# Linear attention and feed-forward joined into one stage by 512 tokens, with the low half of the feed-forward's inner rows on GpSimd

## The reference

```python
# linear attention, 16 heads of 16, over the 64 rows of a sequence
q, k, v = relu(x @ Wq.T + bq), relu(x @ Wk.T + bk), x @ Wv.T + bv
kv    = einsum('bnhd,bnhp->bhdp', k, v)
denom = maximum(einsum('bnhd,bhd->bnh', q, k.sum(axis=1)), 1e-6)
y     = einsum('bnhd,bhdp->bnhp', q, kv) / denom + x
out   = (y - mean(y)) / sqrt(var(y) + 1e-5) * gamma + beta
# feed-forward, 768 inner rows, int weights times 1/127
h   = silu(x @ (w_gate / 127).T) * (x @ (w_up / 127).T)
out = h @ (w_down / 127).T
```

## Time and profile before

| | us |
|---|---|
| median of 3 runs | 2300.51 (2300.44 to 2300.74) |
| the profiled execution's own time | 2298.4 |
| its span, first to last instruction | 2296.7 |
| TensorE busy | 2145.7 (93%) |
| VectorE busy | 1202.0 (52%) |
| ScalarE busy | 1066.5 (46%) |
| GpSimd busy | 483.7 (21%) |
| mean granted TensorE clock | 0.969 |

### The profile page before, as it was taken

The page is one execution under the profiler, slowest core; times in us unless marked ns, Lnnn a source line. Parts: engine busy times, 40 slices in busy tenths (PEclk is TensorE's granted clock), DMA queues, the critical chain, the costliest instruction groups (busy, mean ns, idle before and its releaser), DMA issues. The chain is left out here.

```text
span 2296.7 us, 51145 instructions
## 1 busy us (share of the span) xinstructions
PE 2145.7 (93%) x21377; PEld 1876.0 (82%) x21377; DVE 1202.0 (52%) x3545; ACT 1066.5 (46%) x2411; POOL 483.7 (21%) x365
## 2 busy tenths in 40 slices
PE   6999999999999997845979999999999899999999
PEld 6888989898988896424857888878989889898898
DVE  6655555555555554485345778862786532313311
ACT  4545444545444543203226666653444344444443
POOL 1000000000000000102011212223454454545544
PEclk9999999999999998977989999998999999999999
DMA  4100000000000000000031111010101011011000
GB/s 138 29 20 15 20 15 20 15 20 20 15 20 15 20 2 21 4 11 31 1 102 30 31 30 30 12 39 1 56 1 38 1 38 37 1 38 37 1 10 28
DMA packets 48805, 58.12 MB, mean 25 GB/s; under 512 B 6529, under 2 KB 40129, under 8 KB 48449
## 3 DMA queue, kind: packets, MB, share of 16 engines
q1 hardware_dynamic: 48576, 54.85, 7.6%
HBM read 46.72 MB, written 2.10 MB: 21 GB/s over the span
## 5 line engine op out<-in xcount | busy, mean ns | idle before, releaser
L797 POOL TENSOR_TENSOR moe_h<-moe_hr,moe_h 128x512 fp32r<-128x512 f32 x256 | 361.4, 1412 | 428.0 <-ACT moe_hr L1109 428.0
L1108 ACT ACTIVATE moe_h<-bank,dec_b 128x512 fp32r<-128x512 f32 x256 | 176.4, 689 | 418.9 <-PE bank L83 415.8
L2092 DVE TENSOR_REDUCE lat_neg_max<-bank 128x1 f32<-128x320 f32 x256 | 113.6, 486 | 319.0 <-PE bank L1873 319.0
L83 PE MATMUL bank<-lat_wv,lat_kv_t 128*128 128x256 f32 (+1 forms) x1728 | 264.8, 303 | 10.3 <-ACT lat_v L1967 3.9
L83 PE MATMUL bank<-lat_kv_t,lat_wk 128*128 128x320 f32 x1536 | 256.3, 316 | 0.0
L83 PEld LDWEIGHTS bank<-lat_wv,lat_kv_t 128*128 128x128 f32 x1728 | 224.1, 190 | 33.7 <-ACT lat_v L1967 5.7
L83 PEld LDWEIGHTS bank<-lat_kv_t,lat_wk 128*128 128x128 f32 x1536 | 225.8, 188 | 0.1
L1463 DVE SCALAR_TENSOR_TENSOR x_sb<-bank,moe_xs,x_sb 128x256 f32<-128x256 f32 x96 | 39.8, 477 | 352.0 <-PE bank L966 351.9
L83 PE MATMUL bank<-dec_xt,dec_lo 128*128 128x512 f32 x512 | 202.6, 396 | 0.0
L1981 ACT ACTIVATE lat_p<-bank,lat_neg_max 128x320 f32<-128x320 f32 x256 | 137.0, 535 | 114.0 <-DVE lat_neg_max L2092 114.0
L1569 POOL TENSOR_TENSOR lat_rs_rstdc<-lat_rs_varc,lat_rs_halfc 128x4 f32<-128x4 f32 x16 | 16.2, 1014 | 765.8 <-DVE lat_rs_varc L1561 765.8
(11 more groups left out here) (316 smaller groups left out, 3954.3 us busy)
## 6 DMA issues: line engine op xcount, KB each, us to landing
raw_w<-in_L_ffn_W SPq DMA_DIRECT2D x16, 1024.0 KB, 6.5
lat_ctx_raw<-in_ctx SPq DMA_DIRECT2D x16, 512.0 KB, 4.1
att_ctx_raw<-in_ctx_turned SPq DMA_DIRECT2D x16, 512.0 KB, 3.8
lat_kv_t<-lat_lt SPq DMA_DIRECT2D x32, 128.0 KB, 2.2
out_x<-x_sb SPq DMA_DIRECT2D x4, 512.0 KB, 2.9
x_sb<-in_x SPq DMA_DIRECT2D x1, 1792.0 KB, 14.7
lat_xl_now<-lat_xl SPq DMA_DIRECT2D x7, 256.0 KB, 4.5
lat_raw<-in_L_xattn_Wq SPq DMA_DIRECT2D x1, 1024.0 KB, 7.5
```

The costliest lines, as they stand in the source:

```text
L83: mm = pe.matmul(out, lhs(a, k), rhs(b, k), start=first and k == 0 and n == 0, stop=last and k == KD - 1 and n == 2)
L797: pool.tensor_tensor(h[:, g % 2, 1, :], hr[:, g % 2, :], h[:, g % 2, 0, :].bitcast(F32), ALU.subtract).then_inc(h_lo, 1)
L1108: act.activation(h[:, n % 2, 0, :], h_bank[n % 2][:, :], ACT.Relu, bias=bias).then_inc(h_hi, 1)
L2092: dve.tensor_reduce(neg_max[:, u:u + 1], s_bank[h][:, 0:LK], AX.X, ALU.max, negate=True).then_inc(s_max, 1)
```

## The change

The two stages become one, `linear_feed`. It goes by chunks of four tiles (`PER` = 4, 512 tokens). While chunk c goes through linear attention, chunk c-1 goes through the feed-forward; the last chunk's feed-forward comes at the end alone. The barrier between the stages goes. Every engine's queue is written anew:

```diff
...
+            sp.dma_start(wi[:, :, 0, :], rows(w["L0_ffn_w_gate"])).then_inc(ffn_loads, 16)
+            sp.dma_start(wi[:, :, 1, :], rows(w["L0_ffn_w_up"])).then_inc(ffn_loads, 16)
+            sp.dma_start(wdi[:, :, :], rows(w["L0_ffn_w_down"])).then_inc(ffn_loads, 16)
...
         @block.gpsimd
...
+            def hidden_low(c, h):
+                n = c * NH + h
+                pool.wait_ge(h_hi, n + 1)
+                pool.tensor_tensor(ht[:, 1, h, :], hf[:, n % 2, :], ht[:, 0, h, :].bitcast(F32),
+                                  ALU.subtract).then_inc(h_lo, 1)
+            power_and_shift(norm_l, shift_l, l_shift, 0)
+            pool.wait_ge(ffn_loads, 48)
+            pool.tensor_scalar(wf[:, :], wi[:, :], 1.0 / 127.0, None, ALU.mult).then_inc(gu_float, 1)
             pool.wait_ge(loads, 128)
-            pool.wait_ge(front.xn_ready, NT)
-            pool.tensor_tensor(x_sb[:, :, :], x_sb[:, :, :], beta[:, :].unsqueeze(1).to_broadcast([P, NT, D]),
-                               ALU.add).then_inc(beta_added, 1)
-            pool.wait_ge(consts, 3)
-            norm2.power(pool, 0)
+            add_beta(0)
+            pool.tensor_scalar(wdf[:, :], wdi[:, :], 1.0 / 127.0, None, ALU.mult).then_inc(wd_float, 1)
+            low_weights_up()
+            power_and_shift(norm_l, shift_l, l_shift, 1)
+            norm_y.power(pool, 0)
+            power_and_shift(norm_f, shift_f, f_shift, 0)
+            low_weights_down()
+            for c in range(1, NCH):
+                add_beta(c)
+                for h in range(PER):
+                    hidden_low(c - 1, h)
+                    if h == 1 and c + 1 < NCH:
+                        power_and_shift(norm_l, shift_l, l_shift, c + 1)
+                norm_y.power(pool, c)
+                hidden_low(c - 1, PER)
+                hidden_low(c - 1, PER + 1)
+                power_and_shift(norm_f, shift_f, f_shift, c)
+            for h in range(NH):
+                hidden_low(NCH - 1, h)
...
         @block.tensor
...
+            def gate_up(c, h):
+                n = c * NH + h
+                if n == 0:
+                    pe.wait_ge(gu_lo, 1)
+                if h == 0:
+                    pe.wait_ge(f_lo, 2 * c + 2)
+                for g, (bank, done, freed) in enumerate(((gate_bank, gate_psum, silu_done), (up_bank, up_psum, h_done))):
+                    if n >= 1:
+                        pe.wait_ge(freed, n)
+                    product3(pe, bank[:, :], lambda a, kd: wgu[:, a, kd, g, h * P:(h + 1) * P],
+                             lambda a, kd: ft[:, a, kd, :]).then_inc(done, 1)
+            def down(c, i):
+                n = c * PER + i
+                if n == 0:
+                    pe.wait_ge(wd_lo, 1)
+                if n >= 2:
+                    pe.wait_ge(x_done, n - 1)
+                if i == 0:
+                    pe.wait_ge(h_lo, NH * (c + 1))
+                for h in range(NH):
+                    for j, (a, b) in enumerate(PASSES):
+                        mm = pe.matmul(down_bank[n % 2][:, 0:D], ht[:, a, h, i * P:(i + 1) * P], wd[:, b, h, :],
+                                       start=h == 0 and j == 0, stop=h == NH - 1 and j == 2)
+                mm.then_inc(down_psum, 1)
+            turn_rows(0)
+            pe.wait_ge(loads, 128)
+            queries(0)
             keys_values(0)
-            for t in range(NT):
-                states(t)
-                if t + 1 < NT:
-                    keys_values(t + 1)
-                contexts(t)
+            for c in range(NCH):
+                for i in range(PER + 1):
+                    if c >= 1:
+                        gate_up(c - 1, i)
+                    if i >= 1:
+                        contexts(PER * c + i - 1)
+                    if i < PER:
+                        states(PER * c + i)
+                    if i + 1 < PER:
+                        keys_values(PER * c + i + 1)
+                if c >= 1:
+                    gate_up(c - 1, NH - 1)
+                if c + 1 < NCH:
+                    turn_rows(c + 1)
+                    queries(c + 1)
+                if c >= 1:
+                    down(c - 1, 0)
+                    down(c - 1, 1)
+                if c + 1 < NCH:
+                    keys_values(PER * (c + 1))
+                if c >= 1:
+                    down(c - 1, 2)
+                turn_ffn(c)
+                if c >= 1:
+                    down(c - 1, 3)
+            for h in range(NH):
+                gate_up(NCH - 1, h)
+            for i in range(PER):
+                down(NCH - 1, i)
...
         @block.vector
...
+            rows_stats(0)
+            norm_l.close(dve, 0)
+            dve.wait_ge(loads, 128)
+            dve.wait_ge(consts, 5)
             keys_values(0)
-            for t in range(NT):
-                states(t)
-                if t + 1 < NT:
-                    keys_values(t + 1)
-                contexts(t)
-            dve.wait_ge(y_ready, NT)
-            norm2.gather(dve, lambda t: y[:, t, :], 0)
-            dve.wait_ge(norm2.rstd_ready, 1)
-            dve.wait_ge(beta_added, 1)
-            for t in range(NT + 1):
-                if t < NT:
-                    dve.scalar_tensor_tensor(out=y[:, t, :], in0=y[:, t, :], scalar=norm2.mean[:, t:t + 1], in1=gamma[:, :],
-                                             op0=ALU.subtract, op1=ALU.mult).then_inc(tail, 1)
-                if t >= 1:
-                    dve.wait_ge(tail, t)
-                    dve.scalar_tensor_tensor(out=x_sb[:, t - 1, :], in0=y[:, t - 1, :], scalar=norm2.rstd[:, t - 1:t],
-                                             in1=x_sb[:, t - 1, :], op0=ALU.mult, op1=ALU.add).then_inc(x_done, 1)
+            for c in range(NCH):
+                for i in range(PER + 1):
+                    t = PER * c + i
+                    if c >= 1:
+                        hidden(c - 1, i)
+                    if i >= 1:
+                        contexts(t - 1)
+                    if i < PER:
+                        states(t)
+                    if i + 1 < PER:
+                        keys_values(t + 1)
+                    if i >= 1:
+                        y_row(t - 1)
+                    if i == 0 and c + 1 < NCH:
+                        rows_stats(c + 1)
+                    if i == 1 and c + 1 < NCH:
+                        norm_l.close(dve, c + 1)
+                    if i == PER:
+                        norm_y.close(dve, c)
+                if c >= 1:
+                    hidden(c - 1, NH - 1)
+                scale_rows(c)
+                if c >= 1:
+                    residual(c - 1, 0)
+                    residual(c - 1, 1)
+                if c + 1 < NCH:
+                    keys_values(PER * (c + 1))
+                if c >= 1:
+                    residual(c - 1, 2)
+                ffn_low(c)
+                if c >= 1:
+                    residual(c - 1, 3)
+            for h in range(NH):
+                hidden(NCH - 1, h)
+            for i in range(PER):
+                residual(NCH - 1, i)
...
-STAGES = ["latent_attention", "linear_attention", "feed_forward"]
+STAGES = ["latent_attention", "linear_feed"]
```

More of the change, by code:

```diff
@@ L208, in linear_attention, with setup @@
[L208 to L220 removed]
+    def setup(self, pool, made):
+        pool.memset(self.half[:, :], -0.5).then_inc(made, 1)
@@ new lines, in power_and_shift, with add_beta @@
+            def power_and_shift(norm, shift, ready, c):
+                at = slice(c * PER, (c + 1) * PER)
+                norm.power(pool, c)
+                pool.wait_ge(norm.rstd_ready, c + 1)
+                pool.tensor_tensor(shift[:, at], norm.mean[:, at], norm.rstd[:, at], ALU.mult).then_inc(ready, 1)
+            def add_beta(c):
+                pool.wait_ge(l_xn, PER * (c + 1))
+                at = slice(c * PER, (c + 1) * PER)
+                pool.tensor_tensor(x_sb[:, at, :], x_sb[:, at, :], beta[:, :].unsqueeze(1).to_broadcast([P, PER, D]),
+                                   ALU.add).then_inc(x_beta, 1)
@@ L334, in _, with queries, keys @@
+            def queries(c):
+                for m in range(KD):
+                    act.wait_ge(q_psum, KD * c + m + 1)
+                    act.activation(qt[:, c % 2, m, :], st_bank[m][:, :], ACT.Relu, bias=bq[:, m:m + 1]).then_inc(q_done, 1)
+            def keys(t):
                 act.wait_ge(k_pre, t + 1)
@@ new lines, in gate, with high @@
+            def gate(c, h):
+                n = c * NH + h
+                act.wait_ge(gate_psum, n + 1)
+                if n >= 2:
+                    act.wait_ge(h_done, n - 1)
+                act.activation(silu[:, n % 2, :], gate_bank[:, :], ACT.Silu).then_inc(silu_done, 1)
+            def high(c, h):
+                n = c * NH + h
+                act.wait_ge(h_done, n + 1)
+                if c >= 1 and h == 0:
+                    act.wait_ge(down_psum, PER * c)
+                act.copy(ht[:, 0, h, :], hf[:, n % 2, :]).then_inc(h_hi, 1)
@@ new lines, in hidden, with residual @@
```

(12 more changed lines are left out.)

490 lines of the change are left out of this document (203 added, 287 removed).

## The result

The changed kernel takes 2263.96 us in the median (2263.19 to 2267.51, 4 runs), the kernel before 2300.48 us in the same comparison: a ratio of 0.9847, 95% interval 0.983 to 0.9864. The forecast was 2261 us, range 2246 to 2281. The profiled execution took 2264.27 us.

What follows compares the result with a forecast made beforehand. Bound by turns by TensorE, a three-engine chain, and VectorE with GpSimd and ScalarE. Stage 53.6 + 2 x 45.0 + 42.9 + 29.3 + 4 = 219.8 against 258.9 us, giving 2261 us; 80% range 2246 to 2281.

Steps and rivals of the forecast that it cites:

- full step: In the joined tile loop, TensorE's gate and up pair, contexts, states, keys and values together: 5.7 us.
- c=2: Second of the two iterations with rows, queries and keys to put in between; 45.0 us, normalisation hidden by 2 us.
- c=3: Last joined iteration, without next rows, queries or keys to cover the normalisation; 42.9 us.
- The beginning: First part of the joined stage, c = 0, which nothing covers, GpSimd's queue being in order; 53.6 us.
- The wait of close(1): In c = 0, VectorE's tiny statistics sums wait for GpSimd's low-weight subtraction; 5.3 us, range 0 to 6.9.
- The wait in a step: VectorE waits for GpSimd's low half in each step; 1.0 us (0 to 1.3), hidden as 5.0 under 5.7 us.
- Rival 1: Shared port decides the steps: two VectorE waits a step, 6.6 us under TensorE's 5.7; 2278 us, chance 0.22.
- The waits around the last pair: TensorE waits for ScalarE's last high half and two copies of turned rows before the queries; 2.1 us.
- The clock: TensorE's granted clock falls behind new gaps; 4 us added for two such losses, range 0 to 8.
- Rival 2: Port and clock cost nothing, taking off 5.3 us in c = 0, 2 in c = 3, 4 of clock; 2250 us, chance 0.16.
- Rival 3: ScalarE reloads its table as Silu alternates with Relu, eight loads an iteration, 31 us; 2290 us, chance 0.04.
- Rival 4: In-order queues lay the two halves end to end, 63.8 us an iteration; 2320 us, chance 0.03.

Runs made afterwards that it cites:

- conv_dve: The changed kernel with the two integer weight conversions moved from GpSimd back to VectorE; 2261.4 us, ratio 0.984 to the kernel before.
- early: The changed kernel with gate and up weights loaded first, conversions on VectorE, low-weight subtraction before the tile loop, ScalarE's weight copy before the queries; 2261.49 us.
- spare1: The changed kernel with one unread VectorE product added ahead of each product hf of the first three chunks; stage 232.6 us against 226.7.
- warm: The changed kernel with transposes whose results nobody reads put into TensorE's gaps; 2258.89 us.
- spare3: The changed kernel with three unread VectorE products added ahead of each product hf of the first three chunks; stage 253.3 us against 226.7.

## Why the prediction held, point by point

- **The direction and the mechanism** held. The two halves run side by side; the full step is 5.94 us for my 5.7, and c=2, c=3 came within 0.2 us of their terms. In c=2 that is partly two misses that cancel: its steps took 27.8 us for my 27.0, the wait before the queries and the queries themselves 4.7 for my 5.6. My own terms put TensorE's demand for the normalised rows at 41.8 us and not at 41.5; in c=2 it came at 42.1 and the rows were ready at 40.0 (39.5 forecast), so the cover was 2.2 us for my 2.
- **The beginning was mis-sized**, by 6.9 of the 6.9 us that the stage is over my 219.8; the iterations and the tail, clock included, are over by nothing. The step that failed is the line "I take 2.8, since one operand is read": the conversion took 7.96 us, beyond even the upper bound of 6.9, and the second 4.26 for my 1.4. The weights were ready 16.6 us after the start, not 14; 2.3 us of that is the wait for the third load, which this conversion does not read (up was issued at 917.57 us and took 9.9 us to land, down landed at 929.8). Together 2.6 + 5.2 + 2.9 = 10.7 us; 3.3 of it was absorbed, since my plan had ScalarE's copy, not GpSimd's queue, come last ahead of the subtraction. The low weights ended at 37.8 us for my 30.6; from there to the first gate I had 23.0 us, measured 22.7. conv_dve and early confirm that GpSimd's queue ahead of the subtraction set it: with that queue shortened the beginning fell by 4.1 and by 10.6 us. The prediction named this as what would make the beginning wrong.
- **The wait of close(1)**: 5.3 us forecast; the row takes 6.54 us, 6.38 more than elsewhere; early removes it. The Trainium skill, page "SBUF — State Buffer", section "SBUF: two separate sides", calls the shared port pair an exclusive lock for a whole instruction; the 6.54 and 5.14 us rows and the sums of 1.35 us agree. The rows of 1.33 and 0.15 us inside the integer conversion, and of 0.42 us beside the power, do not: there VectorE did not wait for the end of the GpSimd instruction.
- **The wait in a step**: 1.0 us forecast, 0.93 measured, and hidden. Rival 1, which had two such waits decide the steps, is out: 5.94 us a step and TensorE waits for VectorE nowhere in it. But I had read a row too kindly: the sum into x_sb did not take 1.58 us "once", it took over 1.2 us in 43 of 256 cases of the kernel before. The cover was as thin as the prediction said, and in c=2 thinner than I later took it in spare1.
- **The waits around the last pair**: 2.1 us forecast, 1.58 measured; before the last chunk's down projections 4.3 (31.3 less 27.0), measured 3.79; in the tail 3.0 and 2.92.
- **The clock**: 4 us forecast, 4.2 by warm, most of it in c=1 and the tail. Rival 2 had put the clock and the port at nothing, and is out.
- **Rival 3**, table reloads: the stage has one load, 1283 ns, and the kernel three, as before. The Trainium skill, page "ScalarE: Activation LUTs", section "Table sets: the hidden batching unit", says that cheap functions such as relu and copy are in every set; the trace agrees.
- **Rival 4**, halves end to end: 57 us an iteration was its mark; the longest is 47.7.
- **ScalarE's four rows** took 2.07 us, 590 ns each in the groups by line, for my 1.6. It can have cost the beginning 0.5 us only once, at the feed-forward's rows: at the first rows TensorE had its copies 8.5 us after the start, as forecast, and then waited for the load of beta until 10.6 us, where I had put the loads at 8.5.
- **The total** came nearer than the stage did: 3.0 us off, the stage 6.9. The profiled execution is 5.0 us over my 2259.3: 6.9 of the stage, 1.5 ahead of it, less 3.4 behind it. The rest is the medians: I added 2.1 us to come from that execution to the median, and the median lies 0.3 us below it. None of that was foreseen, and it is luck.

## What to carry to other kernels

When two stages are laid into each other, the middle follows from adding up the busiest engine, and what is left to win is at the ends: here 10.6 us lay in the order of the loads, in which engine converts the weights and in where one long GpSimd instruction falls. Put a long GpSimd instruction that reads two operands from SBUF where VectorE is idle: all 17 VectorE instructions with two SBUF operands that began within one of 1.26 us or more in the changed kernel's joined stage, of four columns or of 256, ended only behind it. The integer conversion and the power did not hold them up so. And moving work from VectorE to GpSimd is worth what VectorE does not lose in waiting: here 16.5 us moved and 14.7 were lost.

## What the runs showed of the hardware that I had not expected

- An integer-to-float multiplication on GpSimd took 7.96 us for 128x3072 (2.6 ns a column) and 4.26 us for 128x1536 (2.8 ns): more than its subtraction of two float operands of the same size, 6.65 us. On VectorE it was 1.76 us for 128x3072.
- A one-input VectorE instruction was held up too: the second conversion, 128x1536, took 0.95 us in conv_dve and 1.83 us in early, where it began 1.33 us into GpSimd's addition of beta and ended 0.8 us behind it. The statistics of 128x256, also of one input, showed nothing of the kind (0.41 us).
- Code that is the same in both kernels differed by steps of 1.3 to 1.6 us between profiled executions, and all but one of these steps go with the granted clock. The windows of the first 40 us, of the kernel before, the changed kernel and spare3, and then one place in the decoder, before and changed:

```profile
0.00:40.00 40.00, 23.21 (x148) 20.78 (x149) 22.31 (x54) 17.58 (x25) 4.77 (x15) 0.96 0.61 197
...
0.00:40.00 40.00, 23.34 (x136) 20.76 (x138) 20.91 (x52) 17.41 (x25) 4.77 (x15) 0.91 0.61 197
...
0.00:40.00 40.00, 23.11 (x154) 20.83 (x155) 23.28 (x57) 17.60 (x25) 4.77 (x15) 1.00 0.60 197
...
1368.00:1378.00 10.00, 9.24 (x122) 7.95 (x123) 5.77 (x26) 5.38 (x12) 1.03 (x1) 0.83 0.19 54
...
1338.50:1348.50 10.00, 9.26 (x140) 7.81 (x144) 7.24 (x29) 6.78 (x16) 1.01 (x1) 1.00 0.18 55
```

The mean granted clock of the first 40 us took three values in the twelve executions of this document. With 1.00 the stage begins at 909.6 to 909.8 us, with 0.96 at 911.7 to 912.1, with 0.91 at 913.2 to 913.7. In the decoder the changed kernel is 1.6 us ahead behind the second pair of windows (clock 0.83 before, 1.00 in the changed kernel) and 1.6 us more behind 1585 to 1600 us (0.74, and 0.80 in the changed kernel). The third step there, 1.3 us around 1980 us, has the clock at 1.00 in both: the kernel before has two low halves of 6.39 us together beside VectorE's subtractions, and TensorE waited 0.88 and 0.22 us for low halves; the longest there in the changed kernel took 2.05 us. Why the clock fell in one execution and not in another is not shown. These steps are why I compare stages rather than single times where a kernel ran once.
